# Relation tables made in the edge MLP's loop, without bias and gate

## The reference, cut to what matters

```python
# block 2, edge MLP
h = concat([x[src], edge_attr]) @ W1 + b1            # 256 wide
h = gelu(layernorm(h) * g1 + be1)
agg = segment_sum(h @ W2 + b2, dst)
u = concat([x, agg]) @ Wu + bu
x = _layernorm(x + (gelu(layernorm(u) * gu + beu) + x))
# block 3, relations: 8 relations, rel is the type of an edge
xw   = einsum('ni,rio->rno', x, W)
msg  = xw[rel, src] + bias_term[rel]
gate = sigmoid(sum(msg * gate_weight[rel], -1) + gate_bias[rel])
agg  = segment_sum(msg * gate[:, None], dst)
x = _layernorm(x + relu(agg + x @ loop_weight))
```

## Time and profile before

| | |
|---|---|
| time, median of 3 runs | 4499.05 us (4494.59 to 4503.68) |
| span of the profiled execution | 5314.6 us; no other time of that execution is given |
| PE busy | 3112.7 us, 59%, 15416 matmuls |
| PE weight loads | 2793.1 us, 53% |
| DVE busy | 2515.0 us, 47%, 5316 instructions |
| ACT busy | 1308.4 us, 25%, 3470 instructions |
| POOL busy | 3165.2 us, 60%, 3335 instructions |

### The profile page before, as it was taken

One profiled execution on the slowest core, in us unless ns is written; L12 is line 12 of the kernel. 1 busy time (PEld: TensorE's weight loads), 2 busy tenths in 40 slices (PEclk: granted clock), 3 DMA queues, 4 the chain that ended last, 5 costly groups with the idle time before them and its releaser, 6 DMA issues. The chain is left out here.

```text
span 5314.6 us, 52198 instructions
## 1 busy us (share of the span) xinstructions
PE 3112.7 (59%) x15416; PEld 2793.1 (53%) x15416; DVE 2515.0 (47%) x5316; ACT 1308.4 (25%) x3470; POOL 3165.2 (60%) x3335
## 2 busy tenths in 40 slices
PE   2666666666377787777871323333332666666666
PEld 2665666566366676666731223323231666666665
DVE  2344444445377878777870111112121454554555
ACT  0010010011267777777760000000000011111111
POOL 5666666663566666666206666666654666666662
PEclk6556556666689888988895566665665565555656
DMA  5444444443444444444241111111112333333331
GB/s 140 128 144 139 151 142 140 151 140 110 138 134 145 147 144 144 143 144 148 81 189 47 48 49 49 50 49 47 52 43 67 97 95 97 99 95 97 98 96 52
DMA packets 284107, 567.22 MB, mean 107 GB/s; under 512 B 108648, under 2 KB 157034, under 8 KB 283802
## 3 DMA queue, kind: packets, MB, share of 16 engines
q0 software_dynamic: 119664, 280.17, 20.3%
q1 hardware_dynamic: 157082, 278.92, 15.4%
q10 hardware_dynamic: 7056, 4.56, 0.3%
HBM read 465.83 MB, written 97.56 MB: 106 GB/s over the span
## 5 line engine op out<-in xcount | busy, mean ns | idle before, releaser
L840 POOL DMA_INDIRECT rows<-gat_table,src_i x1662 | 1568.6, 944 | 861.4 <-issue 464.9
L1593 POOL DMA_INDIRECT rows<-mlp_table,src_i x831 | 789.5, 950 | 527.0 <-issue 303.8
L1254 POOL DMA_INDIRECT rows<-rel_table,rel_i x831 | 783.9, 943 | 494.8 <-issue 343.4
L1129 PE MATMUL p_sum<-rows,hot 128*128 128x133 f32 x3328 | 781.6, 425 | 14.2 <-DVE rows L906 12.5
L1121 PEld LDWEIGHTS p_adc<-adw,hot_t 128*128 128x128 f32 x3328 | 688.1, 314 | 178.0 <-DVE hot_t L880 127.5
L1121 PE MATMUL p_adc<-adw,hot_t 128*128 128x8 f32 x3328 | 678.0, 342 | 147.7 <-DVE hot_t L880 108.4
L1129 PEld LDWEIGHTS p_sum<-rows,hot 128*128 128x128 f32 x3328 | 735.9, 326 | 17.2 <-DVE rows L906 15.6
L1411 PE MATMUL p_sum<-hot,rows 128*128 128x128 f32 x1664 | 324.5, 363 | 715.9 <-DVE hot L1281 365.9
L1411 PEld LDWEIGHTS p_sum<-hot,rows 128*128 128x128 f32 x1664 | 298.6, 272 | 744.3 <-DVE hot L1281 381.2
L1061 ACT COPY sums<-p_sum 128x133 f32<-128x133 f32 x208 | 56.4, 271 | 2211.6 <-DMA rel_index<-rel_i 1902.6
L1889 PE MATMUL p_sum<-hot,rows 128*128 128x128 f32 x3328 | 476.0, 310 | 201.8 <-ACT rows L1799 107.7
(11 more groups left out here) (239 smaller groups left out, 3693.9 us busy)
## 6 DMA issues: line engine op xcount, KB each, us to landing
drow<-in_dst_rows SPq DMA_DIRECT2D x208, 512.0 KB
hot_table<-hot SPq DMA_DIRECT2D x104, 512.0 KB
hot<-hot_table SPq DMA_DIRECT2D x104, 512.0 KB
rows<-gat_table,src_i POOLq DMA_INDIRECT x1662
rel_table<-rows SPq DMA_DIRECT2D x49, 512.0 KB, 2.6
eat<-in_edge_t SPq DMA_DIRECT2D x104, 128.0 KB
rows<-mlp_table,src_i POOLq DMA_INDIRECT x831
rows<-rel_table,rel_i POOLq DMA_INDIRECT x831
```

The source lines that it names most:

```text
L840: pool.indirect_dma_start(out=rows[:, n % RING, t, :], out_offset=None, in_=net.gat_table[:, :], in_offset=bass.IndirectOffsetOnAxis(ap=ne ...
L1129: end = nc.tensor.matmul(p_sum[:, 0:SUMS], hot[:, n % HALF, t, :], rows[:, n % RING, t, 0:SUMS], start=(t == 0), stop=(t == T - 1))
L1254: pool.indirect_dma_start(out=rows[:, n % RING, t, :], out_offset=None, in_=net.rel_table[:, :], in_offset=bass.IndirectOffsetOnAxis(ap=ne ...
L1593: pool.indirect_dma_start(out=rows[:, n % RING, t, :], out_offset=None, in_=net.mlp_table[:, :], in_offset=bass.IndirectOffsetOnAxis(ap=ne ...
```

## The change

**In `mlp_pass`** the relation tables move into the loop. One of the two sum banks is given up: `p_sum` is a single bank, and `pt` becomes a bank of its own. `add_up(n)` therefore waits for `added` of the group before it, and DVE's `add` moves ahead of `pre` in a step. The `rows` ring has 7 slots (`MLP_RING`), not 8, which makes room for `stage`, three buffers of half a table tile. `OfTable` and `Unit.tab` go. At `unit.at + 15` (`TURN_AT`) PE transposes the unit's x into `pt` and DVE copies it into `turned`; at + 16 (`GATE_AT`) PE makes the gate product, DVE adds the gate bias (the result is the logit, no sigmoid). Then, tile by tile, one per step: PE makes half a tile (4 relations) into `pt`, ACT copies it and 4 columns of logits into `stage`, SP stores it; PE makes the other half into the same bank, DVE copies it and its logits, SP stores it. So there are 98 stores instead of 49. No relation bias is added, no gate applied: the table row is x @ W[r] and its logit, 129 numbers.

**In `rel_pass`** the gathered row is 129 numbers. The types of the edges are worked out once from `rel_i` and `src_i`. Per group ACT makes the sigmoid of the logit column (`gates`), DVE makes a one-hot of the relation types (`kinds`, 128x64), multiplies it and the rows (128x1024) by the gates (`weigh`), and adds a second sum. PE's `add_up` moves one step later, DVE's `add` two steps behind; PE makes 8 more matmuls per group, which sum the gates by relation and destination into `p_sum[0:8, 128:256]`. Per node tile `multiply` gets one more matmul, these gate sums times the relation bias.

```diff
+        def part_of(unit, i, q):
+            return 2 * (unit.first + i) + q
+        def staged(h):
+            return stage[:, h % TABS, :].rearrange("p (r f) -> p r f", f=REL)
+        def each_half(fn, q, lag):
+            return [(lambda unit, i=i: fn(unit, i, q) if i < unit.tiles else None, lag + i) for i in range(UNIT)]
 # SP, mlp_pass
+            def store_part(unit, i, q):
+                h, cols = part_of(unit, i, q), slice(q * R // 2 * REL, (q + 1) * R // 2 * REL)
+                sp.wait_ge(s.second_kept if q else s.first_kept, unit.first + i + 1)
+                sp.dma_start(table[unit.first + i:unit.first + i + 1, :, cols].rearrange("t p c -> p (t c)"), stage[:, h % TABS, :]).then_inc(s.stored[h % TABS], 16)
+            stores = in_turn(each_half(store_part, 0, GATE_AT + 1), each_half(store_part, 1, GATE_AT + 2))
 # POOL, mlp_pass
-                wait(pool, s.summed, n - RING + 1)
+                wait(pool, s.summed, n - MLP_RING + 1)
 # DVE, mlp_pass
+            def copy_new(unit):
+                dve.wait_ge(s.new_turned, unit.u + 1)
+                nc.vector.tensor_copy(turned[:, 0:unit.tiles, :], pt[:, 0:unit.tiles, :]).then_inc(s.new_copied, 1)
+            def keep(unit, i, q):
+                h = part_of(unit, i, q)
+                dve.wait_ge(s.tab_product, h + 1)
+                wait(dve, s.stored[h % TABS], 16 * (h // TABS))
+                nc.vector.tensor_copy(staged(h)[:, :, 0:F], pt[:, :, :])
+                nc.vector.tensor_copy(staged(h)[:, :, F], logit[:, i, q * R // 2:(q + 1) * R // 2])
+                dve.drain().then_inc(s.second_kept, 1)
-                drive(sh, [(pre, 0), (add, 3), (scale, 1)], pieces(True))
+                weave(sh, [(add, 3, False), (pre, 0, False)] + [(fn, lag, True) for fn, lag in tables] + [(scale, 1, False)] + [(fn, lag, True) for fn, lag in weights + steps])
 # ACT, mlp_pass: keep as on DVE, with first_kept
+                weave(sh, [(inner_normalise, 9, True), (outer_normalise, NORMED_AT, True), (square, 0, False)] + [(fn, lag, True) for fn, lag in keeps]
+                      + [(inner_root, 7, True), (outer_root, 12, True), (gelu, 1, False), (node_gelu, 10, True), (copy_x, 2, True)])
 # PE, mlp_pass
-                wait(pe, s.added, n - 1)
+                wait(pe, s.added, n)
+            def turn_new(unit):
                 pe.wait_ge(s.normed, unit.u + 1)
+                wait(pe, s.second_kept, unit.first)
                 for i in range(unit.tiles):
                     end = nc.tensor.transpose(pt[:, i, :], net.x[:, unit.first + i, :], net.ident[:, :])
+                end.then_inc(s.new_turned, 1)
+            def fill(unit, i, q):
+                if q:
+                    pe.wait_ge(s.first_kept, unit.first + i + 1)
+                elif i:
+                    pe.wait_ge(s.second_kept, unit.first + i)
+                else:
+                    pe.wait_ge(s.gate_logits, unit.u + 1)
+                four = slice(q * R // 2, (q + 1) * R // 2)
+                nc.tensor.matmul(pt[:, :, :].rearrange("p r f -> p (r f)"), turned[:, i, :], net.rel_w[:, four, :].rearrange("p r f -> p (r f)"),
+                                 start=True, stop=True).then_inc(s.tab_product, 1)
+            turns, firsts, seconds = [(turn_new, TURN_AT), (gate_logit, GATE_AT)], each_half(fill, 0, GATE_AT), each_half(fill, 1, GATE_AT + 1)
-                drive(sh, [(edges, 0), (add_up, 2)], pieces(True))
+                weave(sh, [(edges, 0, False)] + [(fn, lag, True) for fn, lag in turns + seconds] + [(add_up, 2, False)]
+                      + [(fn, lag, True) for fn, lag in pieces(True) + firsts])
 # DVE, rel_pass
+            def kinds(half, given):
+                nc.vector.tensor_tensor(kind[:, half, :, :], tiled(given, T, R), over_tiles(net.iota_row[:, 0:R], T, R), ALU.is_equal)
+                dve.drain()
+            def weighted(slot, half, k):
+                nc.vector.tensor_tensor(kind[:, half, :, :], kind[:, half, :, :], tiled(gate[:, k, :], T, R), ALU.mult)
+                nc.vector.tensor_tensor(rows[:, slot, :, 0:F], rows[:, slot, :, 0:F], tiled(gate[:, k, :], T, F), ALU.mult)
+                return dve.drain()
+            def weigh(n):
+                kinds(n % HALF, types[:, n, :])
+                dve.wait_ge(s.gated, n + 1)
+                weighted(n % RING, n % HALF, n % 2).then_inc(s.weighed, 1)
             def add(n):
                 ...
+                part, gates = net.acc[:, 0, bass.ds(first, P)], net.acc[0:R, 1, bass.ds(first, P)]
                 nc.vector.tensor_tensor(part, part, p_sum[n % 2][:, 0:P], ALU.add)
+                nc.vector.tensor_tensor(gates, gates, p_sum[n % 2][0:R, P:2 * P], ALU.add)
-                drive(sh, [(one_hot, 0), (add, 1)], pieces)
+                drive(sh, [(one_hot, 0), (weigh, 1), (add, 2)], pieces)
 # ACT, rel_pass
+            def gates(n):
+                act.wait_ge(s.gathered[n % RING], landed(sh, n))
+                wait(act, s.weighed, n - 1)
+                nc.scalar.activation(gate[:, n % 2, :], rows[:, n % RING, :, F], ACT.Sigmoid).then_inc(s.gated, 1)
 # PE, rel_pass
+            def sums(k, slot, half):
+                for t in range(T):
+                    nc.tensor.matmul(p_sum[k][0:R, P:2 * P], kind[:, half, t, :], hot[:, half, t, :], start=(t == 0), stop=(t == T - 1))
+                for t in range(T):
+                    end = nc.tensor.matmul(p_sum[k][:, 0:P], rows[:, slot, t, 0:F], hot[:, half, t, :], start=(t == 0), stop=(t == T - 1))
+                return end
             def add_up(n):
                 pe.wait_ge(s.onehot, n + 1)
+                pe.wait_ge(s.weighed, n + 1)
                 wait(pe, s.added, n - 1)
+                sums(n % 2, n % RING, n % HALF).then_inc(s.summed, 1)
+                    nc.tensor.matmul(pu[:, t, :], net.acc[0:R, 1, cols], rb[:, :], start=False, stop=False)   # in multiply
-                drive(sh, [(add_up, 0)], pieces(True))
+                drive(sh, [(add_up, 1)], pieces(True))
```

More of the change, by code:

```diff
@@ L53 @@
 Shapes = namedtuple("Shapes", "N E NT NP NW NG NB NBATCH BN units")
-Unit = namedtuple("Unit", "u first tiles after at tab")
-OfTable = namedtuple("OfTable", "lag")
+Unit = namedtuple("Unit", "u first tiles after at")
 def shapes_of(n, e):
@@ L80, in units_of @@
         at = max(after, at + APART)
-        units.append(Unit(u, first, m, after, at, 0))
+        units.append(Unit(u, first, m, after, at))
         first += m
-    start, end = ng + 2, at + NORMED_AT + 1
-    spread = [start + (end - start) * unit.u // max(1, len(units) - 1) for unit in units]
-    return tuple(unit._replace(tab=max(at, unit.at + NORMED_AT + 1)) for unit, at in zip(units, spread))
+    return tuple(units)
 def least_bases(sh):
@@ L674, in given, with landed @@
     return range(min(T, -(-(sh.E - n * GE) // P)))
-def landed(sh, n):
-    return 16 * sum(len(given(sh, k)) for k in range(n % RING, n + 1, RING))
+def landed(sh, n, ring=RING):
+    return 16 * sum(len(given(sh, k)) for k in range(n % ring, n + 1, ring))
 def tiles_of(unit):
@@ L1445, in slow_window @@
                 pe.wait_ge(s.onehot, v + 1)
-                for t in range(T):
-                    end = nc.tensor.matmul(p_sum[0][:, 0:P], rows[:, 0, t, :], hot[:, 0, t, :], start=(t == 0), stop=(t == T - 1))
-                end.then_inc(s.summed, 1)
+                sums(0, 0, 0).then_inc(s.summed, 1)
             def pieces(fast):
@@ L1585, in _ @@
             for k in range(TABS):
-                wait(sp, s.stored[k], 16 * sum(unit.tiles for unit in sh.units[k::TABS]))
+                wait(sp, s.stored[k], 16 * len(range(k, 2 * sh.NT, TABS)))
         @s.block.gpsimd
@@ L1645, in add @@
                 part = net.acc[:, :, bass.ds(first, P)]
-                nc.vector.tensor_tensor(part, part, p_sum[n % 2][:, 0:2, :], ALU.add)
+                nc.vector.tensor_tensor(part, part, p_sum[:, 0:2, :], ALU.add)
                 dve.drain().then_inc(s.added, 1)
@@ L1739, in evacuate @@
                 nc.vector.tensor_tensor(logit[:, 0:unit.tiles, :], p_gate[:, 0:unit.tiles, :], over_tiles(net.rel_gate_bias[:, :], unit.tiles, R), ALU.add).then_inc(s.gate_logits, 1)
-                dve.wait_ge(s.summed, sums_done(fast))
-                wait(dve, s.stored[unit.u % TABS], 16 * kept_before(unit, TABS))
-                for i in range(unit.tiles):
-                    t = unit.first + i
-                    tab = tab_of(unit, i)
-                    dve.wait_ge(s.tab_product, t + 1)
-                    nc.vector.tensor_tensor(tab, p_tab[t % 2], net.rel_b[:, :, :], ALU.add).then_inc(s.tab_read, 1)
-                    dve.drain()
-                    if i == 0:
-                        dve.wait_ge(s.gate_ready, unit.u + 1)
-                    nc.vector.tensor_tensor(tab[:, 0:by_dve, :], tab[:, 0:by_dve, :], tiled(gate[:, k, i, 0:by_dve], by_dve, F), ALU.mult).then_inc(s.dve_scaled, 1)
@@ L1836, in outer_normalise @@
                 end.then_inc(s.normed, 1)
```

(28 more changed lines are left out.)

169 lines of the change are left out of this document (84 added, 85 removed).

## The result

4558.17 us median (4556.57 to 4560.75, 4 runs) against 4500.74 us (4494.59 to 4503.68, 4 runs): ratio 1.0129, 95% interval 1.0115 to 1.0144. The change makes the kernel 57 us slower.

What follows compares the result with a forecast made beforehand. The prediction took POOL's gather issue to set the pace, with compute close behind in the MLP loop. Terms -76 + 33 + 40 + 5 gave +2 us on 4499, so 4501 us, range 4425 to 4580.

Steps and rivals of the forecast that it cites:

- second rival: Table work in the MLP loop and held gathers in the relation pass all add time: +77, 4576 us, chance 0.22.
- (a): Table phase after the MLP: nine tiles left of 49, 69 us instead of 145, -76 us, bounds -60 and -90.
- (b): MLP loop: added table work on DVE, ACT and PE is mostly hidden, +33 us, bounds 0 and +78.
- (c): Relation pass: added work +10 and gathers held by the multiply +30, together +40 us, bounds 0 and +85.
- The rival on the tail: Table phase: hand-overs bind units 10 to 12, 7 us per tile, gap loses only 45 us: 4532 us, chance 0.05.
- cover of 0.2 us per group: MLP loop: a timed group takes 9.9 us against 9.7 of compute, so 0.2 us of DVE's added 0.56 is hidden.
- The reading of the trace: All passes: in timed runs a gather comes every 1.0 us, not 1.25, explaining the trace's extra 815.6 us.
- The port: Relation pass: the multiply's two SBUF operands hold gathers, 49 to 61 us over the pass, of which +30 was taken.
- (d): End of the relation pass: sigmoid, weighing and 16 further products behind the last landing, +5 us.
- The ring of 7: MLP pass: POOL waits one group sooner for a free buffer, 0 us, at best -10 at the start.
- the path case: Everything in the loop on the path, 4576 us, chance 0.22; its sign was a traced MLP group above 12.1 us.
- The two signs that the prediction is wrong altogether: The relation pass changes by more than 90 us, or span and median move in different directions.

Runs made afterwards that it cites:

- tail_two_banks: The kernel after, with the second half of each table tile of units 10 to 12 put in the bank of the sums: 4537.1 us.
- before_one_bank: The kernel before, with one bank for the MLP's sums instead of two and DVE's add first in its step: 4536.2 us.
- tables_late: The kernel after, with every piece of the relation tables placed behind the MLP loop: 4785.0 us.
- add_after_scale_late: The kernel after, with DVE's add one step earlier, behind scale, and all table pieces placed behind the MLP loop: 4751.7 us.
- rel_gate_psum: The kernel after, with the relation pass's gates in a PSUM bank of their own instead of SBUF: 4529.4 us.
- first trace: The original trace of the unchanged kernel before, from which the prediction was made: span 5314.6 us against a median of 4499.05.
- second trace: The unchanged kernel before, traced once more as a follow-up: span 4493.4 us.
- keep_on_act: The kernel after, with the copy of the second half of each table tile made by ACT instead of DVE: 4554.7 us.

## Why the prediction was right or wrong

The time, 4558 us, lies in the range. The forecast of "no change", +2 us, was wrong (measured +57), and so was its own narrow range (4475 to 4530). What happened is nearest to the second rival, everything in the loop on the path (4576 us), though not by all of its mechanism: its +78 for the loop came about (+82.8), its +70 for the relation pass did not (+32.6). The sum came nearest by luck: its terms were off by +21 us in (a) and +5 in (b) and by -37 in (c). In the forecast itself nearly all errors point one way, +21 in (a), +50 in (b), -7 in (c), and the time lies in the range only because that reached to the outer cases.

- **(a) Table phase**: -76 forecast, -55.3 measured, just outside its bound of -60. The mis-sized term is the tile: 4.4 us forecast, 5.85 measured, 9 x 1.45 = 13 us. I took the product's 1.0 us from rows in which PE was kept busy; in a serial chain through one bank it is busy 52.7 of 90.1 us, the granted clock is 0.53 and the product takes 2.08. I had that as the outer bound ("every tile 6 us, PE at its lower clock") and chose the warm one. Another 5 us went to one small copy (below); the last 3 us were not looked for. The rival on the tail was right in kind, one bank and its hand-overs, and tail_two_banks shows it.
- **(b) The MLP's loop**: +33 forecast, +82.8 measured, beyond the bound of +78. Two steps. First, "the earlier place of `add` costs nothing, since it stands before `pre`, whose product PE makes after those same sums" is the step that failed outright: +34 to +36 us (before_one_bank, tables_late), gone when the add moves (add_after_scale_late). I looked at what stands behind the add and not at what DVE must finish ahead of it. Second, the table work: 33 forecast, 48.4 measured. There is a slip in the sum (0.56 - 0.2 is 0.36 and not 0.33, so 32 us and not 29), but the error is the cover of 0.2 us per group. No cover is left: in 800 us of before DVE waits for gathered rows 0.4 us in all, and PE waits only for gelu. Compute ends this pass, its last sum coming 32 us behind the last gather before and 68 after. My figure for DVE without any cover, 48, meets the 48.4 partly by luck: DVE's busy time grew by 999.1 - 963.3 = 35.8 us only, and the rest is idle time that I had no term for.
- **The reading of the trace**: that a timed gather comes every 1.0 us was wrong (1.25). The group of 9.9 us that I drew from it was nearly right all the same, by luck: (2164.7 - 1122.8) / 103.9 = 10.0 us, which is 8 x 1.25, the gathers' own pace.
- **(c) The relation pass**: +40 forecast, +32.6 measured. The port, +30, is the measured term by itself; the work, +10, was 0 (rel_gate_psum). The size came out right by a weaker argument than it looks: I averaged the wait over random starts (0.47 to 0.59 us) and took off what pauses would swallow. Nor was L1722 the only operation in the MLP's loop with both operands in SBUF: L1714 and L1716 are such too, and in before_one_bank the gather that starts at 1602.60, beside L1716, takes 1.07 us. In the relation pass there are no pauses, and the starts are not random. The multiply is released by the last gather's landing, so it stands at nearly the same place against the next gathers, 0.7 to 0.9 us ahead of the start of one in 102 of 104 groups (0.87 in the timeline above), and holds it by 0.22 us there and 33 / 104 = 0.32 us in the mean.
- **(d)** +5 forecast, +2.1 measured.
- **The ring of 7**: 0 forecast, 0 measured.
- **Of the signs to look for**: from the start of the last sum to the first relation gather it was not 73 us but 2370.0 - 2276.0 = 94; the traced group stayed under 12.1 (10.5 us, by the gathers), so that sign pointed away from the path case that came true, but it rested on the disturbed first trace; gathers of 1.2 us, one per group, came as described. The two signs that the prediction is wrong altogether came true as written: against the first trace the relation pass went from 1180 to 1069.6 us, more than 90, and the span fell to 4559.0 us while the median rose. Against the second trace the relation pass changes by 32.6 us and both span and median rise (+65.6 and +57). So what these signs found was the first trace, from which the terms had been read.

## What to carry to other kernels

When work moves into a loop whose busiest engine is near 90% busy and waits for no gather, price it at no less than the full busy time of the busiest engine, and look at what every moved instruction stands behind in its queue, not only at who waits for it. A second buffer that is given up need not cost anything, if the instruction that frees the first one is placed right where its data comes ready. Hold the numbers of one trace against the median first; where they are far apart, the pauses in it are not those of a timed run. And an elementwise operation beside gathers wants one operand in PSUM.

## What was not expected of the hardware

A POOL memset and a small DVE copy, from the phase of after:

```profile
2303.86 5.43 POOL L1659 MEMSET acc_t<- 128x6400 f32 x1
2303.96 5.35 DVE L1791 COPY stage<-logit 128x4 f32<-128x4 f32 x1
```

The copy of 4 numbers per partition within SBUF takes 0.16 us elsewhere and ends here with the memset; the copy from PSUM that starts beside the memset ahead of it took its usual 0.69. PE's next product waits for it, so by the trace it costs some 5 us of the phase. In tail_two_banks the same two memsets lie over a small copy of 1.16 us and a TENSOR_SCALAR of 128x3 of 3.49 us (0.17 elsewhere). In keep_on_act, where ACT makes the copies, the copy beside the second memset takes its usual 0.20 us, PE's wait of 6.08 us behind it is gone, and that phase is 9.2 us shorter; a DVE operation off the chain of the tiles (TENSOR_SCALAR of 128x3) takes 4.47 us there. In all three traces such a small DVE operation ends within 0.03 us of the memset, while other DVE operations beside it (0.56 and 0.68 us in tail_two_banks) and ACT's copies do not wait for it. I did not run a kernel with the memset elsewhere, so the 5 us are read from the traces.
